# Indirect transfers of POOL behind waits on PE: four per tick of the dense pass, pairs in the attention layers

## The reference

```python
# block 0, GIN, twice: agg = segment_sum(x[src], dst); h = x + agg; relu(h @ wa + ba) @ wb + bb; then h @ wl + bl
# block 1, relational: W[r] = sum_b w_comp[r, b] * bases[b]; out = sum_r segment_sum over edges of type r (x[src]*w) @ W[r]
# block 2, GCN on 10,000-node style weights: y = x @ W.T; out = segment_sum(norm * y[row], col) + bias
# block 3, three attention layers:
h = h_in @ Wl
a = (h @ asl)[src_f] + (h @ adl)[dst_f] + ea_f @ (Wel @ ael)     # edges and a self loop per node
a = where(a > 0, a, 0.2 * a); alpha = softmax of a over the edges of one dst
out = segment_sum(h[src_f] * alpha, dst_f) + bl
out = (out - mu) * rsqrt(var + 1e-05) * gl + bel
```

## Time and profile before

| | us |
|---|---|
| median of 3 runs | 4961.03 (4953.85 to 4983.9) |
| the profiled execution | 4922.33 |
| its span, first to last instruction | 4920.6 |
| PE busy | 3040.0 (62%) |
| DVE busy | 2637.4 (54%) |
| ACT busy | 2245.0 (46%) |
| POOL busy | 1923.9 (39%) |

### The profile page before, as it was taken

One profiled execution on the slowest core, in us unless ns is written; L12 is line 12 of the kernel. 1 busy time (PEld: TensorE's weight loads), 2 busy tenths in 40 slices (PEclk: granted clock), 3 DMA queues, 4 the chain that ended last, 5 costly groups with the idle time before them and its releaser, 6 DMA issues. The chain is left out here.

```text
span 4920.6 us, 67479 instructions
## 1 busy us (share of the span) xinstructions
PE 3040.0 (62%) x18099; PEld 2447.4 (50%) x18099; DVE 2637.4 (54%) x8154; ACT 2245.0 (46%) x5893; POOL 1923.9 (39%) x1994
## 2 busy tenths in 40 slices
PE   1183008997887787785664039991089991058675
PEld 1062006775443454443563039990079881057665
DVE  2083008998444565796562017770047881068876
ACT  0072008886111344675453027770057770057765
POOL 6605760000553563663664730007700007700465
PEclk8596559998776787997776569895588875586655
DMA  3293016665554343454663237772256763255443
GB/s 116 69 333 115 12 38 210 222 223 178 149 154 124 88 117 112 127 172 146 177 202 121 63 102 244 219 225 63 59 183 205 226 197 84 66 171 196 142 133 96
DMA packets 419338, 723.50 MB, mean 147 GB/s; under 512 B 76431, under 2 KB 137908, under 8 KB 418606
## 3 DMA queue, kind: packets, MB, share of 16 engines
q1 hardware_dynamic: 350990, 610.53, 38.1%
q0 software_dynamic: 63040, 107.35, 8.7%
q10 hardware_dynamic: 5024, 2.30, 0.2%
HBM read 428.65 MB, written 321.10 MB: 152 GB/s over the span
## 5 line engine op out<-in xcount | busy, mean ns | idle before, releaser
L684 POOL DMA_INDIRECT msgs<-t_gat,row_i x591 | 566.9, 959 | 1149.7 <-DMA t_gat<-t_hn 923.1
L1739 PE MATMUL t_p_q<-mean_col,t_nsq 128*128 128x1 f32 x2352 | 341.5, 266 | 288.7 <-issue 248.0
L1739 PEld LDWEIGHTS t_p_q<-mean_col,t_nsq 128*128 128x128 f32 x2352 | 350.7, 228 | 301.1 <-issue 301.1
L2246 ACT ACTIVATE t_nnt<-t_p_nt,cxt 128x512 f32<-128x512 f32 x294 | 200.6, 682 | 592.8 <-remote 356.8
L700 POOL DMA_INDIRECT dg_g_ring<-t_xw,src_i x197 | 189.4, 961 | 648.2 <-DVE slot_id L1203 572.6
L2083 PE MATMUL t_p_nt<-ident,t_nh 128*128 128x128 f32 x1176 | 219.5, 318 | 264.7 <-issue 179.2
L1732 PE MATMUL t_p_nh<-wx,t_nnt 128*128 128x132 f32 x1568 | 258.0, 314 | 185.8 <-issue 127.3
L2006 POOL DMA_INDIRECT out_rows<-t_hn,own_i x197 | 201.2, 1021 | 401.9 <-issue 335.3
L1732 PEld LDWEIGHTS t_p_nh<-wx,t_nnt 128*128 128x128 f32 x1568 | 222.1, 216 | 186.7 <-issue 186.1
L2083 PEld LDWEIGHTS t_p_nt<-ident,t_nh 128*128 128x128 f32 x1176 | 160.0, 164 | 280.6 <-issue 261.9
L828 PE MATMUL de_p_o<-wc,de_hh 128*128 128x128 f32 x1568 | 219.3, 284 | 112.1 <-DVE de_r L955 86.6
(11 more groups left out here) (411 smaller groups left out, 8704.4 us busy)
## 6 DMA issues: line engine op xcount, KB each, us to landing
t_gat<-t_hn SPq DMA_DIRECT2D x296, 264.0 KB
t_nh<-t_gat SPq DMA_DIRECT2D x294, 264.0 KB
t_x<-de_x SPq DMA_DIRECT2D x196, 256.0 KB
t_ah<-t_gat SPq DMA_DIRECT2D x150, 264.0 KB
t_gat<-de_h SPq DMA_DIRECT2D x98, 264.0 KB
t_xw<-in_x_map SPq DMA_DIRECT2D x28, 903.0 KB
de_xt<-in_x_t SPq DMA_DIRECT2D x98, 256.0 KB
t_xn<-t_x SPq DMA_DIRECT2D x98, 256.0 KB
```

Source lines behind the costliest of these rows:

```text
L684: self.nc.gpsimd.indirect_dma_start(out=self.msgs[:, c, 0:width], out_offset=None, in_=table, in_offset=bass.IndirectOffsetOnAxis(ap=idx[: ...
L1739: last = self.nc.tensor.matmul(p_q[:, j:j + 1], sq[:, j * D:(j + 1) * D], self.mean_col[:], start=True, stop=True)
L2246: nc.scalar.activation(nnt[:, g % 2], p_nt[:], ACT.Identity, bias=bias).then_inc(act_nt, 1)
```

## The change

In the dense pass POOL's 140 gathers, 197 scatters and 33 gathers are cut into groups of four (PACE); ahead of each group POOL waits until PE's tick counter `pe_a` has reached the number of transfers already issued, divided by four, plus one, and at most 98. The first 24 gathers and the row gathers are as before. In the attention layers the gathers go in pairs (STEP); ahead of each pair POOL waits for the node groups (`pe_nt`) or slot groups (`pe_at`) that `after_items` finds in the plan: one item of the plan per pair, counted from two ticks ahead of the layer's first weights part, and never later than two ticks ahead of the weights of the pair's batch.

```diff
+PACE = 4
+STEP = 2
@@ slot_gathers
+        begun = self.dense_begun
+        done = [0]
+
+        def after_ticks(ops):
+            wait(pool, begun, min(done[0] // PACE + 1, DG))
+            done[0] += ops
+
+        def targets(chunks):
+            for c in range(chunks.start, min(chunks.stop, USED), PACE):
+                group = range(c, min(c + PACE, chunks.stop, USED))
+                after_ticks(len(group))
+                self.resident_gather(self.dst_i, a["x"], D, self.got, group)
...
-        self.resident_gather(self.dst_i, a["x"], D, self.got, range(FIRST, FIRST + EVERY * COPIES))
+        targets(range(FIRST, FIRST + EVERY * COPIES))
         pool.wait_ge(self.x_copied, 16 * COPIES)
         for c in range(USED):
+            if c % PACE == 0:
+                after_ticks(min(PACE, USED - c))
             nc.gpsimd.indirect_dma_start(
...
-        self.resident_gather(self.dst_i, a["x"], D, self.got, range(FIRST + EVERY * COPIES, CHUNKS))
+        targets(range(FIRST + EVERY * COPIES, CHUNKS))
@@ dense_part
+            self.dense_begun = s["pe_a"]
@@ phase_gats
+            first_tick = [min(t for t, (n, a, w) in enumerate(plan) if w is not None and w[0] == layer) - 2 for layer in range(L)]
+            piece_tick = {}
+            for t, (n, a, w) in enumerate(plan):
+                if w is not None and w[1] is not None:
+                    piece_tick.setdefault((w[0], w[1]), t)
+
+            def after_items(layer, b, count):
+                seen, t, what, value = 0, first_tick[layer], "nodes", 0
+                while seen < count and t < piece_tick[layer, b] - 2:
+                    n, a, w = plan[t]
+                    if n is not None and n < NODES:
+                        seen, what, value = seen + 1, "nodes", n + 1
+                    if a is not None and a[1] <= AG:
+                        seen = seen + 1
+                        if n is None and a[1] > 0:
+                            what, value = "edges", a[0] * AG + a[1]
+                    t += 1
+                return what, value
...
-                        self.resident_gather(self.row_i, self.th[layer], XW, got[b], range(2 * r0, 2 * r1))
+                        for c in range(2 * r0, min(2 * r1, USED), STEP):
+                            what, value = after_items(layer, b, c // STEP)
+                            if what == "nodes":
+                                wait(pool, pe_nt, value)
+                            else:
+                                wait(pool, pe_at, value)
+                            self.resident_gather(self.row_i, self.th[layer], XW, got[b], range(c, min(c + STEP, 2 * r1)))
```

## The result

The changed kernel takes 4202.17 us (median of 4 runs, 4173.81 to 4223.38) against 4972.47 for the kernel before (4 runs, 4953.85 to 4987.73): a ratio of 0.8449, 95% interval 0.8387 to 0.851. The forecast was 4040 with a range of 3820 to 4400. The profiled execution of after is the highest of its four, 4223.38 (span 4221.6), against a span of 4920.6 before: 699 us in these two traces, 770 in the medians. Ratios and their intervals leave out a run that is over 1.5% above the fastest of its kernel, which here is one run alone, the profiled one of best (4032.85).

The account below looks back on a forecast made before the run. Signals between engines, late while POOL streams indirect transfers, were taken to bound the dense pass and attention layers. Gains of 427+193+176+129 = 925 us from the 4961 median gave 4040 us, range 3820 to 4400.

Parts of the forecast that it names:

- term (b): Dense pass, 65 paced ticks without a copy: hold-up taken as 0.4 us per four (0 to 2.25), 26 us.
- term (a): Dense pass, 28 ticks with a copy: paced transfers share full DMA engines, 1.05 us a tick, 29 us.
- the anchor: Relational and GCN phases already run groups of four behind PE: no visible loss in one, 4.5 us per eight in the other.
- term for node and slot ticks: Layers 0 and 1: at 1.475 us per gather, pairs make node and slot ticks 64 us dearer, bounds 0 to 111.
- shared wait values: Layer 2: capped waits leave gathers of each batch as streams, costing 30, 40 and 55 us, 125 of 254.
- They cost nothing: Layer 2: a pair takes 2.5 us against node ticks of 3.42, so pairs add no time.
- Nothing else moves: From 1210 to 2637 us and in the output scatters after 4600 the code is the same, so no change.
- No hold-up when spaced: Rival, chance 0.12: only layer 2's streams and the layers' starts cost; gain near 1140, 3820 us.
- Spacing too tight: Rival, 0.20: in layers 0 and 1 pairs outlast node ticks, long waits return; dense pass pays 2.25 per four; 4400 us.
- Transfers stretched by DVE: Rival, 0.02: transfers beside DVE last as long as the longest gather, 2.24 us with the gap; 4720 us.
- No change: Rival, 0.04: the delay is a price per transfer, 1.3 us each, which spacing only spreads; 4960 us.
- Slower: Rival, 0.04: each pair starts the delay anew, POOL waits on late PE signals, 5.5 us per paced tick; 5600 us.

Follow-up runs that it names:

- best: Changed kernel with each dense transfer behind its own signal and layer 2 gathers in threes: 3996.61 us on a late chip (before 4964.88), ratio 0.8045.
- a_again: The changed kernel itself run again, on a chip where signals are prompt: 3479.54 us against 3394.97 for the kernel before, ratio 1.0255.
- best2: As best, but each attention-layer gather also waits for its own signal: 3939.65 us on the second late chip (before 4928.25), ratio 0.7968.

## Why the prediction was right, and where it was not

**The loss and its cause: right, with a limit that the trace of before couldn't show.** 482, 257, 260 and 254 us by ticks; 483, 239, 274 and 245 by the chips on which the streams cost nothing. That signals are late because POOL issues back to back, and more so the longer it does, stands by fours, eights, singles and streams on late chips, and by the recorded semaphores. That it happens at all was taken for a property of the kernel, and it is one of the chips that it ran on. That the first comparison ran on the kind on which the change wins was luck: on the other kind the same forecast would have met a loss of 2.6%. By what road streams on POOL hold up signals stays open.

**Dense pass, term (b): failed.** I took 0.4 us for a tick's hold-up, by the relational phase, and 2.25 as the upper bound. Forecast gain 427, bounds 307 to 482, measured 1150.9-854.2 = 297, just outside. After loses 854.2-665.2 = 189 us against the same kernel on a prompt chip, where I had 29+26 = 55. From its first product at 58.6 to 233 us it makes 25 ticks of 7.0 us, where a_again makes 29 of 6.2 from 52 us on, all but one with a copy: 25x0.8, some 20 us. That is near the 29 of term (a) by luck alone. Term (a) priced transfers that share the DMA engines with the copies, and a_again has the same transfers beside the same copies, in ticks no longer than those without; the 20 us are late signals. Some 17 us more go in one tick, which starts at 833.0 and lasts 23.3 us beside the 16 row gathers, a stream that I had left unspaced and called hidden; best and best2 have it too, as ticks of 26.6 and 26.4 us. The rest, some 150 us over 72 ticks, is 2.1 a tick, close to the GCN phase's 2.25, where I had taken 0.4. The threshold that I named (ticks over 8.7 us refute (b)) was just reached: from 233 us to the last tick 643 us go for 73 ticks, 8.8 each, 8.6 without the long one. The step behind it was the anchor.

**The anchor: failed.** "No loss that shows" in the relational phase was read from DVE's busy share of a 200 us stretch. Against prompt chips relational and GCN phase together are 71 to 79 us longer on late ones, the GIN passes 168 to 200, the output scatters 51 to 80. These phases, in groups of four behind PE, pay too (how much of it is late signals and how much the lower clock is not shown); I took the stretch in which it shows least.

**Layers 0 and 1: 193 and 176 forecast, 150 and 172 measured.** The term for node and slot ticks was 64 us a layer, within 0 to 111; against prompt chips it is 93 in both (524.0-430.8, 575.7-483.0). It isn't the pair that outlasts the tick, as I priced it: on prompt chips the same pairs take 430.8 and 483.0 against 434.8 and 473.6 with streams. It is PE's lower clock and its longer idle time, in layer 0 of best2 47 and 32 us; the clock's price I left out. Best2's single gathers take off 14 and 7, no more than traces of one code differ by. The late start's 20 us in layer 1 I can't separate.

**Layer 2: 129 forecast, 118 measured (861.5 to 743.6 us to the end), with the wrong reason for part of it.** I took the shared wait values for streams, and priced them by late signals. They are also late batches: on a prompt chip, where no signal is late, they alone cost 375.8-274.9 = 101 us, of which the output scatters give 17 back. So that 129 and 118 lie close is in part luck. Two lines of after's trace show the end of that stream and what PE did meanwhile:
```profile
3863.73 0.94 POOL L686 DMA_INDIRECT msgs<-t_gat,row_i  x1 [0.30 <-issue]
3842.22 1.84 PE L1756 MATMUL t_p_q<-mean_col,t_nsq 128*128 128x1 f32 x8 [34.01 <-issue]
```
"They cost nothing" of the pairs before the cap was the wrong sentence: 27, 52 and 75 items lie before the three batches' weights and 32, 64 and 98 pairs are wanted. (Of batch 1, 24 gathers share node 275, not 22.)

**"Nothing else moves": right.** The phases between took 38 us more in after's trace, by which I had doubted it. GIN 2 alone is at 372.0, 398.3, 372.8, 400.8 and 380.8 us in five executions on late chips of one and the same code for that phase, and at 287 to 291 on prompt ones: it is the spread between executions on late chips.

**The rivals.** No hold-up when spaced (3820): refuted for fours, nearly true of single transfers in the dense pass. Spacing too tight (4400): no waits of 21 us came back in layers 0 and 1; of that rival only the dense pass's price came true, 2.1 a tick near its 2.25. Transfers stretched by DVE: refuted, after's dense gathers take 997 ns and its scatters 1021. The 3100 ns of the "DVE blocks DMA" trap of the Trainium skill (SBUF — State Buffer) are not seen here; whether any of DVE's operations beside them runs in the two-port mode that it asks for, the traces don't tell. No change: it came true on prompt chips for the dense part. That was not for the reason that I gave, and not by engines taking queues in turn (the Trainium skill, DMA: Bandwidth & Descriptors, "SWDGE vs HWDGE vs iDMA"), since the same stream starves the rest on late chips at a DMA share of 0.09: that statement is about transfers, and what is late here are signals between PE, ACT and DVE. Slower: what happens on prompt chips is 2.6%, through batches that come late, a mechanism that I had given no chance. The change's own wait turns into a late input, which is the first thing to ask of any wait that is added ahead of a producer.

## What to carry to other kernels

On some chips indirect transfers on POOL hold up the signals between the other engines, by far more than their share of the DMA, and by more the longer the burst: give each a wait of its own on a signal that comes anyway, spread over the tick, and not one wait to four. Look for the short streams that are left: 16 gathers without a wait cost 17 to 20 us here. Count what is due before each deadline against what the pacing lets through; a paced producer must still keep the consumer's rate. And time such a change on more than one chip before keeping it: best and best2, with single dense transfers and threes in layer 2, take 0.80 of the time where signals are late and the same time (0.9994) where they are prompt, while the change as made wins the one and loses the other.

## What the runs showed of the hardware

- Chips differ in this by nearly half the kernel's time: the same program takes 3392.69, 3394.51 and 3394.97 us on three chips, 4928.25 and 4964.88 on two (medians of 7 to 19 runs, those of one chip within 1.3% of each other), and POOL's scatters follow each other at 1.27 us on either kind.
- On late chips a semaphore update between PE, ACT and DVE comes after the end of its instruction by up to 17.5 us in a stream of scatters (405.18 to 422.67) and by up to 2.9 beside fours; with POOL silent, and on prompt chips with the same stream, by 0.03 at most.
- On late chips the loss per burst is 0.2, about 2 and 7.5 us for transfers spread over a tick, in fours and in eights, and in a stream the dense pass makes 3 ticks in 335 us.
- Phases in groups of four behind PE take 27 to 110 us longer on late chips, each with 197 transfers.
